# First layer of a four-layer network: butterfly products inside the attention's steps, and one block for the feed-forward

## What is computed

```python
def butterfly(y, weights, dim):          # weights: (9, 256, 2, 2), dim = 512
    lead = y.shape[:-1]
    for stage in range(weights.shape[0]):
        s = 2 ** stage
        nb = dim // (2 * s)
        yr = y.reshape(*lead, nb, 2, s)
        a, b = yr[..., 0, :], yr[..., 1, :]
        w = weights[stage].reshape(nb, s, 2, 2)
        na = w[..., 0, 0] * a + w[..., 0, 1] * b
        nb2 = w[..., 1, 0] * a + w[..., 1, 1] * b
        y = jnp.stack([na, nb2], axis=-2).reshape(*lead, dim)
    return y
h = jnp.einsum('bsd,dh->bsh', x, W_exp) + b_exp          # 128 -> 512
h = butterfly(h, up_weights, 512)
h = jax.nn.gelu(h + up_bias, approximate=False)
h = butterfly(h, down_weights, 512)
y = jnp.einsum('bsh,hd->bsd', h, W_con) + b_con          # 512 -> 128
return y + down_bias
```

## Time and profile before

| | |
|---|---|
| runs shown, us | 4325.3, 4332.54, 4337.08 (median 4332.54) |
| the profiled execution, us | 4317.83, its span 4315.8 |
| TensorE clock granted, mean of the span | 0.914 of full |
| TensorE busy | 3521.4 us (82%) |
| VectorE busy | 2596.1 us (60%), 6282 instructions |
| ScalarE busy | 2106.1 us (49%) |
| GpSimd busy | 1741.8 us (40%), 1927 instructions |
| DMA | 224.58 MB, 52 GB/s over the span |

### The profile page before, as it was taken

How to read it: one execution, slowest core, us unless ns; L and a number is a source line. 1 busy time by engine, 2 the same in 40 slices (tenths; PEclk the granted TensorE clock), 3 DMA queues, 4 the chain that set the end, 5 groups by cost and what they waited for, 6 DMA issues and landing times. The chain is left out here.

```text
span 4315.8 us, 78729 instructions
## 1 busy us (share of the span) xinstructions
PE 3521.4 (82%) x26908; PEld 2546.5 (59%) x26908; DVE 2596.1 (60%) x6282; ACT 2106.1 (49%) x5647; POOL 1741.8 (40%) x1927
## 2 busy tenths in 40 slices
PE   5888807655999979999996888885999999995581
PEld 2556603343666656666664888873777777774460
DVE  3666672442666646666664666663888888885233
ACT  4666704453556644444444444445666666661120
POOL 3554541312666653332320000002666666672406
PEclk7999958876999999999998999996999999997795
DMA  3777720012000000000001000001222222223122
GB/s 110 205 197 188 187 93 0 9 26 53 1 1 1 1 11 1 1 2 2 2 1 40 0 0 0 0 0 44 77 76 73 73 77 75 77 77 108 59 69 62
DMA packets 232672, 224.58 MB, mean 52 GB/s; under 512 B 59209, under 2 KB 176905, under 8 KB 232074
## 3 DMA queue, kind: packets, MB, share of 16 engines
q1 hardware_dynamic: 225642, 206.52, 16.8%
q0 software_dynamic: 4096, 8.40, 0.6%
q10 hardware_dynamic: 2592, 5.26, 0.3%
HBM read 166.10 MB, written 54.00 MB: 51 GB/s over the span
## 5 line engine op out<-in xcount | busy, mean ns | idle before, releaser
L2211 DVE TENSOR_TENSOR_SCAN a_h<-a_dA,a_dBu_psum 128x512 f32<-128x512 f32 x512 | 596.0, 1205 | 165.2 <-issue 104.4
L1216 POOL TENSOR_SCALAR a_probs<-a_probs,a_row_inv 128x128 f32<-128x128 f32 (+1 forms) x512 | 381.3, 762 | 278.3 <-DVE a_row_inv L1202 278.3
L2168 POOL TENSOR_TENSOR a_h<-a_h,main_g 128x512 f32<-128x512 f32 x256 | 383.5, 1500 | 270.6 <-DVE a_h L2211 260.6
L1714 DVE SCALAR_TENSOR_TENSOR m_acc<-m_o_psum,m_gate,m_acc 128x128 f32<-128x128 f32 x992 | 297.9, 347 | 116.3 <-PE m_o_psum L1678 115.9
L1935 PE MATMUL a_dBu_psum<-a_B_diag,a_dt_u_turned 64*128 64x128 f32 x4096 | 316.9, 289 | 20.6 <-DVE a_h L2211 19.8
L1678 PEld LDWEIGHTS m_o_psum<-m_values,m_hidden 128*128 128x128 f32 x2048 | 313.4, 197 | 30.0 <-ACT m_hidden L1696 2.6
L1670 PE MATMUL m_h_psum<-m_x,m_keys 128*128 128x256 f32 x1024 | 327.4, 410 | 0.0
L1696 ACT ACTIVATE m_hidden<-m_h_psum 128x256 f32<-128x256 f32 x512 | 196.6, 384 | 264.0 <-PE m_h_psum L1670 264.0
L190 POOL TENSOR_TENSOR main_g<-main_g,main_s 128x512 f32<-128x512 f32 x28 | 43.9, 1599 | 696.5 <-ACT main_g L173 696.5
L1541 POOL TENSOR_TENSOR r_position_q<-r_turned_q 128x512 f32<-128x512 f32 x128 | 160.0, 1272 | 388.8 <-DVE r_turned_q L1586 388.8
L1678 PE MATMUL m_o_psum<-m_values,m_hidden 128*128 128x128 f32 x2048 | 313.9, 279 | 0.0
(11 more groups left out here) (540 smaller groups left out, 8148.3 us busy)
## 6 DMA issues: line engine op xcount, KB each, us to landing
main_g<-a_b_c_rows SPq DMA_DIRECT2D x256, 256.0 KB, 3.1
a_band_rows<-main_g SPq DMA_DIRECT2D x64, 512.0 KB, 3.4
a_B<-a_band_rows SPq DMA_DIRECT2D x192, 128.0 KB, 3.2
a_A<-a_band_rows SPq DMA_DIRECT2D x192, 128.0 KB, 3.0
f_x_rows<-f_zero ACTq DMA_DIRECT2D x16, 320.0 KB, 8.8
f_x_expert<-f_x_rows SPq DMA_DIRECT2D x16, 320.0 KB, 2.8
f_y_rows<-f_y_expert SPq DMA_DIRECT2D x16, 320.0 KB, 2.2
f0b_stage_w<-L_ffn_up_weights SPq DMA_DIRECT2D x9, 512.0 KB, 4.3
```

The source lines that it names most:

```text
L1216: ins = nc.gpsimd.tensor_scalar(pr[:, h % NPR, tile[t]], pr[:, h % NPR, tile[t]], rinv[:, p % NST, q:q + 1], None, ALU.mult)
L1714: ins = nc.vector.scalar_tensor_tensor(out=acc[:, t, :], in0=o, scalar=gate[:, t, e:e + 1], in1=acc[:, t, :], op0=ALU.mult, op1=ALU.add)
L2168: tt(h[:, r, :, :], h[:, r, :, :], Cs[:, g % NCS, :, :], ALU.mult).then_inc(hc_pool, 1)
L2211: nc.vector.tensor_tensor_scan(flat, dA[:, M % NDA, q, k, :, :].rearrange("p n t -> p (n t)"), db[:, 2 * (g % 2) + k, :], 0.0, ALU.mult, A ...
```

## The change

The butterfly's stages are computed by VectorE during the attention. A class Butterfly holds the matrices and lists 162 operations: 18 half stages, alternating between up (6 operations on the matrix and 6 on the one-row bias) and down (6). In each step p < 64 of the attention, VectorE takes up to three operations of the list, two between the group loop and keep_band and one behind keep_band; the list is empty behind step 53. Each operation waits for the one before it, and the first of a half stage from the third on waits for its weights. Weights and matrices for the beginning are loaded in the attention's setup block; the other 16 weight tables are issued by SP between its band writes and windows, behind write(9), (11), (15), (17), (21), (23) and so on to (53), each after the operations of two half stages before have ended. The bias's operations go from GpSimd to VectorE. W_con comes transposed from the host, so that block f0t is gone, and the blocks f0b and f0c with it. l0_ffn is one block for all eight chunks: bias matmuls and transposes first, then the same order of raising and lowering, with two more waits for buffers (y_out, y_mm) where the loop had barriers. Two unused helper functions go.

The core of the diff (removed lines of l0_ffn left out):

```diff
+class Butterfly:
+    F, ST = 512, 9
+    def __init__(self, scope, d):
+        F = self.F
+        self.d = d
+        self.up, self.up_bias = scope.sb("up", [P, 2, F]), scope.sb("up_bias", [1, 2, F])
+        self.down = scope.sb("down", [P, 2, F])
+        self.w = scope.sb("stage_w", [P, 2, 2 * F])
+        self.tmp, self.bias_tmp = scope.sb("tmp", [P, F]), scope.sb("bias_tmp", [1, F])
+        self.bias_up = scope.sb("bias_up", [P, F // P])
+        self.bias_out = scope.sb("bias_out", [P, 2])
+        self.ops = []
+        for h in range(2 * self.ST):
+            i, k = h // 2, h % 2
+            for n in range(6):
+                for what in ("down",) if k else ("up", "up_bias"):
+                    self.ops.append((h, what, self.ST - 1 - i if k else i, i, n))
+    def first_of(self, h):
+        return sum(1 for op in self.ops if op[0] < h)
+    def loads(self):
+        d = self.d
+        return [(self.up[:, 0, :], d["W_exp"]), (self.down[:, 0, :], d["W_conT"]),
+                (self.up_bias[:, 0, :], d["b_exp"].rearrange("(a n) -> a n", a=1)), (self.bias_up[:], column(d["up_bias"])),
+                (self.bias_out[:, 0:1], column(d["b_con"])), (self.bias_out[:, 1:2], column(d["down_bias"]))]
+    def weights(self, h):
+        i, k = h // 2, h % 2
+        src = self.d["down_weights"][self.ST - 1 - i] if k else self.d["up_weights"][i]
+        return self.w[:, h % 2, :], src.rearrange("k r c -> (k r c)").unsqueeze(0).broadcast_to([P, 2 * self.F])
+    def turn(self, eng, op):
+        h, what, st, i, n = op
+        rows = 1 if what == "up_bias" else P
+        both = {"up": self.up, "up_bias": self.up_bias, "down": self.down}[what]
+        size, nb = 2 ** st, self.F // (2 * 2 ** st)
+        def split(t):
+            return t.rearrange("p (m r n) -> p m r n", r=2, n=size)
+        y, o = split(both[0:rows, i % 2, :]), split(both[0:rows, 1 - i % 2, :])
+        m = split(self.tmp[0:rows, :]) if what != "up_bias" else split(self.bias_tmp[:])
+        w = self.w[0:rows, h % 2, :].rearrange("p (m n r c) -> p m n r c", m=nb, n=size, r=2, c=2)
+        r = n // 3
+        def weight(cc):
+            return w[:, :, :, cc, r] if what == "down" else w[:, :, :, r, cc]
+        if n % 3 == 0:
+            return eng.tensor_tensor(m[:, :, r, :], weight(1), y[:, :, 1, :], ALU.mult)
+        if n % 3 == 1:
+            return eng.tensor_tensor(o[:, :, r, :], weight(0), y[:, :, 0, :], ALU.mult)
+        return eng.tensor_tensor(o[:, :, r, :], o[:, :, r, :], m[:, :, r, :], ALU.add)
...
+                    for dst, src in tables.loads() + [tables.weights(0), tables.weights(1)]:
+                        sp.dma_start(dst, src, allow_slow_non_contiguous=True).then_inc(tables_in, 16)
...
+                    sp.wait_ge(tables_in, 16 * (len(tables.loads()) + 2))
...
+                ops = iter(enumerate(tables.ops))
+                def turn_table():
+                    n, op = next(ops, (None, None))
+                    if op is None:
+                        return
+                    h = op[0]
+                    if h >= 2 and n == tables.first_of(h):
+                        dve.wait_ge(weight_in[h % 2], 16 * (h // 2))
+                    if n:
+                        dve.wait_ge(turned_op, n)
+                    tables.turn(nc.vector, op).then_inc(turned_op, 1)
...
+                    if p < NQ:
+                        turn_table()
+                        turn_table()
                     if band_of(p) is not None:
                         keep_band(band_of(p))
+                    if p < NQ:
+                        turn_table()
...
+                def put_weights(h):
+                    sp.wait_ge(turned_op, tables.first_of(h - 1))
+                    dst, src = tables.weights(h)
+                    sp.dma_start(dst, src).then_inc(weight_in[h % 2], 16)
+                halves = iter(range(2, 2 * tables.ST))
+                due = [next(halves)]
+                def write_and_load(n):
+                    write(n)
+                    while due[0] is not None and (tables.first_of(due[0] - 1) - 1) // 3 <= n - 6:
+                        put_weights(due[0])
+                        due[0] = next(halves, None)
                 for n in range(4):
                     write(n)
                 for b in range(NSEQ):
                     for j in range(3):
                         windows(b, j)
                     if b + 1 < NSEQ:
-                        write(4 * b + 4)
-                        write(4 * b + 5)
+                        write_and_load(4 * b + 4)
+                        write_and_load(4 * b + 5)
                     windows(b, 3)
                     if b + 1 < NSEQ:
-                        write(4 * b + 6)
-                        write(4 * b + 7)
+                        write_and_load(4 * b + 6)
+                        write_and_load(4 * b + 7)
+                assert due[0] is None
...
+    up, dn, upb = tables.up[:, 1, :], tables.down[:, 1, :], tables.up_bias[:, 1, :]
...
+        with nc.Block() as block:
+            @block.tensor
+            def _(pe):
+                def raise_(k):
+                    for f in range(NF):
+                        if k:
+                            pe.wait_ge(acted, NF * (k - 1) + f + 1)
+                        nc.tensor.matmul(hp[:, f, :], up[:, f * P:(f + 1) * P], xn[:, k * W:(k + 1) * W], start=True,
+                                         stop=True).then_inc(up_mm, 1)
+                def lower(k):
+                    if k >= 2:
+                        pe.wait_ge(y_out, k - 1)
+                    for f in range(NF):
+                        pe.wait_ge(acted, NF * k + f + 1)
+                        ins = nc.tensor.matmul(yp[:, k % 2, :], down[:, f, :], hid[:, k % 2, f, :], start=f == 0,
+                                               stop=f == NF - 1)
+                    ins.then_inc(y_mm, 1)
+                pe.wait_ge(made, 1)
+                for f in range(NF):
+                    nc.tensor.matmul(tp[:, 1, f:f + 1], upb[:, f * P:(f + 1) * P], one[:], start=True,
+                                     stop=True).then_inc(biased, 1)
+                for f in range(NF):
+                    nc.tensor.transpose(tp[:, 0, f * P:(f + 1) * P], dn[:, f * P:(f + 1) * P], c["ident"][:]).then_inc(turned, 1)
+                raise_(0)
+                pe.wait_ge(kept, 2)
+                for k in range(NCH):
+                    if k + 1 < NCH:
+                        raise_(k + 1)
+                    lower(k)
+            @block.scalar
+            def _(act):
+                act.wait_ge(kept, 1)
+                for k in range(NCH):
+                    if k >= 2:
+                        act.wait_ge(y_mm, k - 1)
+                    for f in range(NF):
+                        act.wait_ge(up_mm, NF * k + f + 1)
+                        nc.scalar.activation(hid[:, k % 2, f, :], hp[:, f, :], ACT.Gelu,
+                                             bias=bias_up[:, f:f + 1]).then_inc(acted, 1)
+            @block.vector
+            def _(dve):
+                nc.vector.memset(one[:], 1.0).then_inc(made, 1)
+                nc.vector.tensor_tensor(bo[:], tables.bias_out[:, 0:1], tables.bias_out[:, 1:2], ALU.add).then_inc(made, 1)
+                dve.wait_ge(biased, NF)
+                nc.vector.tensor_tensor(bias_up[:], bias_up[:], tp[:, 1, 0:NF], ALU.add).then_inc(kept, 1)
+                dve.wait_ge(turned, NF)
+                nc.vector.tensor_copy(down[:].rearrange("p c n -> p (c n)"), tp[:, 0, :]).then_inc(kept, 1)
+                dve.wait_ge(made, 2)
+                for k in range(NCH):
+                    dve.wait_ge(y_mm, k + 1)
+                    nc.vector.tensor_scalar(g_out[:, k * W:(k + 1) * W], yp[:, k % 2, :], bo[:], None, ALU.add).then_inc(y_out, 1)
...
+    "L0_ffn_W_con",
...
-        l0_attention(nc, c, part("L0_attn"), x, d["x"], xn, s, g)
-        l0_ffn(nc, c, part("L0_ffn"), xn, g)
+        with Scope(nc, "f0") as f:
+            tables = Butterfly(f, part("L0_ffn"))
+            l0_attention(nc, c, part("L0_attn"), tables, xn, s, g)
+            l0_ffn(nc, c, tables, xn, g)
```

More of the change, by code:

```diff
@@ L265, in gate_and_norm @@
         q.barrier()
-def load_padded_columns(nc, scope, pairs):
-    with Scope(nc, scope.name + "_pad") as s:
-        zeroed, landed = s.sems("zeroed landed")
-        with nc.Block() as block:
-            @block.gpsimd
-            def _(pool):
-                for i, (dst, _) in enumerate(pairs):
-                    nc.gpsimd.memset(dst, 0.0).then_inc(zeroed, 1)
-            @block.sync
-            def _(sp):
-                sp.wait_ge(zeroed, len(pairs))
-                for dst, src in pairs:
-                    v = src.rearrange("(j g d) -> g d j", j=4, g=4)
-                    for g in range(4):
-                        sp.dma_start(dst[32 * g:32 * g + 8, :], v[g], allow_slow_non_contiguous=True).then_inc(landed, 16)
-                sp.wait_ge(landed, 64 * len(pairs))
-        s.barrier()
```

(13 more changed lines are left out.)

151 lines of the change are left out of this document (7 added, 144 removed).

## The result

The changed kernel took a median of 4229.75 us (4 runs, 4227.44 to 4230.03) against 4328.92 us (4319.81 to 4337.08) for the kernel before: a ratio of 0.9774, 95% interval 0.9757 to 0.9792, so 98 us less (90 to 105). The prediction was 4278 us, range 4224 to 4307: the sign and the range hold, the size is 48 us off.

What follows compares the result with a forecast made beforehand. The butterfly behind the first layer's attention was taken as a stage in series, costing in full. Terms: -104.3 - 8.0 + 20.8 + 19.5 + 3.6 + 13 + 0.5 = -54.9, giving 4278 us, range 4224 to 4307.

Steps and rivals of the forecast that it cites:

- Parts 1 and 2: Behind the first layer's attention: the serial butterfly stage goes, gaining 104.3 us; the feed-forward loop becomes one block, gaining 8.0.
- Part 3: Attention steps 0 to 53: three VectorE table operations each, 162 in all, taken as exclusive of GpSimd's operations.
- Kind 3: Attention steps with p % 4 = 3: three table operations push back GpSimd's mask chain, 1.6 us a step, 20.8 in all.
- Kind 0: Attention steps with p % 4 = 0: table operations delay the reciprocal TensorE waits for, 1.5 us a step, 19.5 in all.
- Kinds 1 and 2 and the first steps: Attention steps with p % 4 = 1 or 2, 2.6 us in all, plus 1 us for steps 0 to 2.
- The clock, +13 us: Attention: TensorE's idle time after kind 3 grows from 1.79 to 3.4 us, bringing more 1.2 GHz stretches, 13 us.
- Part 4: Queues and transfers: 16 loads on SP's queue hidden by GpSimd's chain, weights asked for two steps ahead; setup 0.5 us.
- setup: Attention's setup: eight loads join behind Wo and may end after VectorE, 0 to 2 us, taken as 0.5.
- The second rival: Attention: no collision with the masks, only kind 0's third operation and the setup cost; 4227 us, chance 0.20.

Runs made afterwards that it cites:

- one input from SBUF: Changed kernel with each of the 162 operations replaced by a row sum over 256 elements of one tensor, tables unmultiplied: 4240.9 us, ratio 0.9757 to the kernel before.
- masks first: Changed kernel with GpSimd's mask_heads behind the sequence's first mask_bands instead of ahead: 4201.8 us, ratio 0.973; the same order in the kernel before: 4295.4 us, 0.993.
- no weight loads: Changed kernel without the 16 later weight loads, its operations reading whatever table is there: 4228.2 us, ratio 0.9774 to the kernel before.
- the kernel with both finds: Changed kernel with mask_heads behind the first mask_bands and kind 0's third table operation moved to kind 1: 4199.16 us, ratio 0.9703 to the kernel before.

## Why the prediction was right in sign and too high

**Parts 1 and 2 were right.** The stage behind the attention went to 3.77 us (predicted 4.9) and the feed-forward to 57.6 (59.5): -105.5 and -10.0 where the sum had -104.3 and -8.0. The loop alone, put back, costs 12.2 + 2.0 us.

**Part 3 named the places and over-priced them; these are the terms that failed.** Predicted 3.6 + 20.8 + 19.5 = 43.9 us, measured by the steps 15.3.
- *Kind 3, "each pushes it back by its own length", 1.6 us.* Measured 0.67. The mechanism is shown (one input from SBUF: 0.00; a wide output alone: no stretch). But the three operations of 0.59, 0.61 and 0.46, 1.66 us in all, push GpSimd by 0.66 together. I had read the earlier trace rows as two engines taking turns without overlap, and the earlier trace rows as too thin. A push of 0.10 on an operation of 0.41, as in the earlier trace rows, is nearer to the 0.15 to 0.31 for each operation here. The Trainium skill (SBUF — State Buffer, Who interferes with whom) has the shared pair held for the whole instruction. Who collides with whom it says rightly here: a VectorE operation with two inputs collided with GpSimd's masks, a reduction with one did not, and either engine can be the one that waits. A hold of whole instructions would have given about the 1.6 predicted, and the runs don't show it. What part of an instruction is exclusive wasn't tried.
- *Kind 0, "+0.9 where GpSimd masks", 1.5 us.* Measured 0.51, the third operation alone. The two ahead of keep_band did meet the masks, but kept their 0.61 and 0.60 us; GpSimd waited in their place, off the path. The prediction took VectorE as the one that waits, and didn't ask which engine it would be. That the cost was lower came from the order of instructions: with the masks first, VectorE does wait there, and the price is 0.94, close to the 0.9.
- *Kinds 1 and 2 and the first steps, 3.6 us.* Nothing to be seen in kinds 1 and 2 (7.27 and 6.78).

**The clock, +13 us, was wrong, and so was its premise.** The idle time of 1.79 us was to grow to 3.4; it is 1.80 in the kernel after. The late mask B holds TensorE up earlier instead: it waits 0.5 to 1.2 us in front of the matmuls that add B, so that the delay comes as a second wait and not as a longer one. Of the two traces of the changed kernel none shows a stretch at 1.2 GHz in the attention; the two of the kernel before show two and eight. The kernels with table work and the shipped order of masks have none to two. The place was right: 16 of the 18 such stretches in all the attentions profiled begin in kind 0, behind kind 3's wait (the other two in step 1), and the three kernels with the masks first have none. How many come is open: I took a longer idle time as the cause on the strength of one stretch, and the unchanged kernel's spread is larger than the term.

**Part 4 was right**: the loads cost nothing (no weight loads), VectorE waits for none, and they land in 6.8 us (median), against the two steps of lead. In the page of after, the list of DMA issues:

```profile
f_stage_w<-L_ffn_up_weights SPq DMA_DIRECT2D x9, 512.0 KB, 6.8
```

**The sum.** Up to the end of the first layer, and against the profiled execution, the terms miss by 12.1 (kind 3), 12.9 (kind 0), 3.6 (the rest of part 3), 16.0 (clock: +13 predicted, -3.0 found, the two stretches that are gone), 1.2 and 2.0 (parts 1 and 2) and 0.3 (setup), together 48.1. Against that stand 1.8 us lost before the first changed instruction and 0.4 that no term holds: -54.9 - 48.1 + 2.2 = -100.8. The untouched later layers of this pair then took 13.1 us more, which no term had, so that the two profiles differ by 87.7; the medians of the runs differ by 99.2. The second rival's 4227 us came nearest, but its reason, no collision, is not what the chip does: more than half of the cost (8.7 of 15.3 us) is a collision.

**The rows that show the collision at a glance** are groups of instructions of one line, GpSimd's masks (mean ns behind the busy time), in the attention of before and then of after:

```profile
L772 POOL TENSOR_SCALAR_AFFINE_SELECT a_A<-a_A 128x512 f32<-128x512 f32 x253 | 140.6, 580 | 47.3 <-DMA a_A<-a_band_rows 37.8 <-POOL a_A L772 0.4
L772 POOL TENSOR_SCALAR_AFFINE_SELECT a_B<-a_B 128x512 f32<-128x512 f32 x126 | 63.1, 524 | 33.7 <-DMA a_B<-a_band_rows 33.7
...
L790 POOL TENSOR_SCALAR a_q_masked<-a_q,a_mask,a_shift_q_masked 128x256 f32<-128x256 f32 x56 | 30.3, 555 | 0.0
```

```profile
L843 POOL TENSOR_SCALAR_AFFINE_SELECT a_A<-a_A 128x256 f32<-128x256 f32 x252 | 149.8, 617 | 32.7 <-DMA a_A<-a_band_rows 23.2 <-POOL a_A L843 0.4
L843 POOL TENSOR_SCALAR_AFFINE_SELECT a_B<-a_B 128x512 f32<-128x512 f32 x126 | 72.6, 599 | 47.8 <-DMA a_B<-a_band_rows 47.7
...
L861 POOL TENSOR_SCALAR a_q_masked<-a_q,a_mask,a_shift_q_masked 128x256 f32<-128x256 f32 x56 | 36.9, 672 | 0.0
```

The same kinds of instructions take 9.2 + 9.5 + 6.6 = 25 us more, and only the 8.7 that fall into kind 3's chain are paid for.

## What to carry to other kernels

Work that stands in series behind a phase can be spread over the idle time of the phase's engines for a seventh of its price (15 of 109 us here), if each place is priced by what waits there: ahead of a copy that TensorE doesn't need at once it was free, ahead of a reciprocal that it does need it cost its full length. When VectorE operations with two inputs from SBUF are put beside GpSimd's, look at which of the two engines carries the critical chain at that moment, since either of them may be the one that waits. Which one it is can turn with the order of instructions: masks first gained 2.6 us a sequence in kind 3, and in kind 0 it made VectorE wait, at a cost of 0.9 us, where GpSimd had waited at none.

## What was not expected of the hardware

- Three VectorE operations (1.66 us in all) delay GpSimd's chain by only 0.66 us. In the other order the delay can be longer than one instruction: an operation of 0.6 us takes 1.60 beside back-to-back affine_selects, two of which began after it.
- An operation with one row of 256 elements costs what one with 128 rows does (0.59 to 0.61 us). Beside the masks too: as the second operation behind a delayed one, in kind 0 of the kernel with both finds, it takes 0.79 to 0.80 us on one row (8 sequences) and 0.80 on 128 (2 sequences).
- The number of stretches at 1.2 GHz in the same attention was two in one execution of the kernel before and eight in another, on another chip, and with it kind 0's median went from 6.88 to 7.82.
- The later layers, whose code is the same, took some 20 us longer on one chip than on the others (3615 to 3622 us against 3588 to 3601).
